# Second attention's causal masks in 32-row pieces on TensorE instead of whole 128-row products

## What is computed

```python
def _L1_attn_ref(x, w_qkv, w_proj):          # x: (16, 256, 128), H = 16, D = 8
    qkv = x @ w_qkv
    q, k, v = jnp.split(qkv, 3, axis=-1)     # then (B, H, T, D)
    att = jnp.einsum('bhqd,bhkd->bhqk', q, k) / sqrt(D)
    causal = jnp.tril(jnp.ones((T, T), dtype=bool))
    att = jnp.where(causal[None, None], att, jnp.finfo(att.dtype).min)
    att = jax.nn.softmax(att, axis=-1)
    y = jnp.einsum('bhqk,bhkd->bhqd', att, v)
    return y.transpose(0, 2, 1, 3).reshape(B, T, C) @ w_proj
```

## Time and profile before

| what | value |
|---|---|
| median of 3 runs | 992.38 us (991.43 to 995.08) |
| the profiled execution | 995.66 us, of which the span of instructions is 993.5 us |
| PE busy | 738.8 us (74%) |
| DVE, ACT, POOL busy | 646.1, 616.5, 457.2 us |
| mean granted TensorE clock | 0.861 of full speed |

### The profile page before, as it was taken

One profiled execution on the slowest core, in us unless ns is written; L12 is line 12 of the kernel. 1 busy time (PEld: TensorE's weight loads), 2 busy tenths in 40 slices (PEclk: granted clock), 3 DMA queues, 4 the chain that ended last, 5 costly groups with the idle time before them and its releaser, 6 DMA issues.

```text
span 993.5 us, 21325 instructions
## 1 busy us (share of the span) xinstructions
PE 738.8 (74%) x8182; PEld 570.7 (57%) x8182; DVE 646.1 (65%) x1190; ACT 616.5 (62%) x1139; POOL 457.2 (46%) x484
## 2 busy tenths in 40 slices
PE   6757777989888990577944777787888888888670
PEld 4445555878878880344632445555766766666540
DVE  5766655767667543777566555475777687688537
ACT  6653545766767462675632444575778878788765
POOL 5476653243443553110005665223566756666632
PEclk8769779999999996678875878698999999999965
DMA  9711112011111115200004222200111111111062
GB/s 312 303 45 54 62 54 60 20 53 31 47 46 39 50 44 149 66 1 2 1 1 156 89 83 69 75 12 23 33 39 38 44 34 39 39 34 31 19 186 85
DMA packets 62357, 63.81 MB, mean 64 GB/s; under 512 B 7378, under 2 KB 52322, under 8 KB 62132
## 3 DMA queue, kind: packets, MB, share of 16 engines
q1 hardware_dynamic: 53300, 44.02, 15.1%
q0 software_dynamic: 8960, 18.43, 5.7%
HBM read 31.88 MB, written 30.55 MB: 63 GB/s over the span
## 4 chain that ended last, share of the span: by engine, by line
PE 33%; ACT 19%; DVE 18%; issue 16%; POOL 8%; another core or an unknown queue 3%; DMA 2%; SPq 0%; ACTq 0%; POOLq 0%; DVEq 0%
POOL xs L1877 6%; PE bank L721 4%; ACT arena L1220 4%; ACT L881 3%; PE bank L786 3%; PE bank L798 3%; PE bank L675 3%; PE bank L528 2%; PE bank L691 2%; DVE arena L1737 2%; DVE arena L1644 2%; DVE arena L1624 2%; DVE arena L1642 1%; PE bank L800 1%
## 5 line engine op out<-in xcount | busy, mean ns | idle before, releaser
L1896 POOL DMA_INDIRECT ys<-arena x152 | 172.7, 1136 | 175.3 <-ACT arena L1149 56.1
L1877 POOL DMA_INDIRECT xs<-arena x128 | 134.0, 1047 | 74.3 <-issue 33.6
L1220 ACT ACTIVATE arena<-bank 128x512 f32<-128x512 f32 x192 | 98.9, 601 | 84.8 <-PE bank L786 59.0
L1737 DVE TENSOR_REDUCE arena<-bank 128x2 bf16<-128x512 f32 (+1 forms) x192 | 119.2, 683 | 41.7 <-PE bank L759 36.8
L661 PE MATMUL bank<-arena 128*128 128x128 bf16 x608 | 105.8, 220 | 6.4 <-DVE arena L1589 3.3
L662 PE MATMUL bank<-arena 128*128 128x128 bf16 x608 | 105.7, 220 | 0.0
L663 PE MATMUL bank<-arena 128*128 128x128 bf16 x608 | 105.7, 219 | 0.0
L881 ACT ACT_TABLE_LOAD x72 | 92.4, 1283 | 1.3
L1725 DVE SCALAR_TENSOR_TENSOR arena<-arena,bank 128x512 bf16<-128x512 bf16 x64 | 46.0, 745 | 72.1 <-ACT arena L1193 68.8
L721 PE MATMUL bank<-arena 128*128 128x256 f32 x256 | 68.5, 416 | 0.9 <-issue 0.9
L661 PEld LDWEIGHTS bank<-arena 128*128 x608 | 60.2, 99 | 9.4 <-issue 6.5
(11 more groups left out here) (236 smaller groups left out, 2051.5 us busy)
## 6 DMA issues: line engine op xcount, KB each, us to landing
xs<-arena SPq DMA_DIRECT2D x19, 516.0 KB, 11.1
arena<-xs SPq DMA_DIRECT2D x38, 258.0 KB
arena<-ys SPq DMA_DIRECT2D x32, 256.0 KB, 5.0
arena<-in_MF SPq DMA_DIRECT2D x8, 512.0 KB
ys<-arena POOLq DMA_INDIRECT x152
arena<-in_x SPq DMA_DIRECT2D x8, 256.0 KB, 5.2
arena<-in_W SPq DMA_DIRECT2D x8, 256.0 KB, 2.7
xs<-arena POOLq DMA_INDIRECT x128
```

Of the source, the lines that this page charges most:

```text
L1220: act(PT[kt_][:, i, gs[0]:gs[0] + len(gs), :], bank_of["s2", b, n, i][:, :].rearrange("p (g q) -> p g q", q=w), ACT.Exp, scale=8 ** -0.5). ...
L1737: red(negM[b % 2][:, u, 32 * i + gs[0]:32 * i + gs[0] + len(gs)], kv_, op=ALU.max, negate=True).then_inc(m_max.sem, 1)
L1877: eng.indirect_dma_start(xs[l][:, :], bass.IndirectOffsetOnAxis(ap=slot_i[l][:, m:m + 1], axis=0), xrow[:, t, :], None).then_inc(rows_move ...
L1896: eng.indirect_dma_start(ys[l][:, :], bass.IndirectOffsetOnAxis(ap=yid[g % 4][:, j:j + 1], axis=0), y[:, 128 * j:128 * j + 128], None).the ...
```

## The change

The mask of a bank is no longer one matmul with 128 rows and 128 columns of the array. It is added in pieces: 32 rows (those of head group i, so that the four banks use the four strips of rows) by 32 columns of the array (32 of the output's partitions), and only over the columns that have anything masked for these partitions. With the order of tokens above that makes five pieces in `s1_four` (widths 32, 64, 32, 64 and 128 in each block; the third and fourth are for the same 32 output partitions) and four in `s2_four` (32, 64, 96 and 128). The counting up of `m_s1` or `m_s2` hangs on the last piece of each bank. The two mask constants hold other patterns, side by side in `masks`, of the same size; they depend on the partition modulo 32 alone. All else is the same.

```diff
+S1_MASKS = ((96, 96, 192, 32), (64, 64, 192, 64), (0, 0, 96, 32), (0, 64, 128, 64), (32, 0, 64, 128))
+S2_MASKS = ((32, 32, 192, 32), (0, 0, 192, 64), (64, 0, 32, 96), (96, 0, 0, 128))
...
-        identb, trib, onesb, negb, negtb = (sb(128, BF16) for _ in range(5))
+        identb, trib, onesb = (sb(128, BF16) for _ in range(3))
+        masks = sb(256, BF16)
...
+            def masks_added(k, i, w, w0, parts):
+
+                r = slice(32 * i, 32 * i + 32)
+                kv_ = k[:, :].rearrange("p (n c) -> p n c", c=w)
+                for q, c, m, width in parts:
+                    j = mm(kv_[q:q + 32, :, w0 + c:w0 + c + width], identb[r, r], bc(masks[r, m:m + width], 1, [32, 512 // w, width]),
+                           start=False, stop=False)
+                return j
...
                 for i, k in four:
-                    kv_ = k[:, :].rearrange("p (n c) -> p n c", c=w)
-                    mm(kv_[:, :, w - 128:w], identb, bc(negb, 1, [128, len(gs), 128]), start=False).then_inc(m_s1.sem, 1)
+                    masks_added(k, i, w, w - 128, S1_MASKS).then_inc(m_s1.sem, 1)
...
                 for i, k in four:
-                    kv_ = k[:, :].rearrange("p (n c) -> p n c", c=w)
-                    mm(kv_[:, :, 0:128], identb, bc(negtb, 1, [128, len(gs), 128]), start=False).then_inc(m_s2.sem, 1)
+                    masks_added(k, i, w, 0, S2_MASKS).then_inc(m_s2.sem, 1)
...
-                for o, i in ((identb, ident), (negb, negm_c), (negtb, negm_r)):
+                for o, i in ((identb, ident), (masks[:, 0:128], negm_c), (masks[:, 128:256], negm_r)):
...
-           np.where(later, -1e30, 0.0), one * (8 - np.arange(8)), one * (16 - np.arange(16)),
-           one * (128 * np.arange(64)), one * np.arange(80), np.where(later.T, -1e30, 0.0), one * i[:, None],
+           np.where(one * (i < 96) + (i - 96 < i[:, None] % 32) > 0, -1e30, 0.0), one * (8 - np.arange(8)), one * (16 - np.arange(16)),
+           one * (128 * np.arange(64)), one * np.arange(80), np.where(one * ((i < 64) + (i >= 96)) + (i - 64 > i[:, None] % 32) > 0, -1e30, 0.0), one * i[:, None],
```

1 line of the change is left out of this document (removed).

## The result

The changed kernel takes 1024.17 us (1021.29 to 1024.9, 4 runs), the kernel before, beside it, 992.84 us (991.43 to 995.08, 4 runs): ratio 1.032, 95% interval 1.028 to 1.037. It is slower by 3%, where the prediction had it faster by 0.9% and a range up to 998.

What follows compares the result with a forecast made beforehand. No engine was full; TensorE was busy 74% of the span and had 33% of the chain. Gains of 9.9 and 2.1 us, 9 after deductions, took 995.66 to 986.7 us, and 3.3 us for the median gave 983.5; range 976 to 998.

Steps and rivals of the forecast that it cites:

- The cost of a round after: Mask rounds at 2.4 GHz, four blocks: `s2_four` 0.41 us for 0.87, `s1_four` 0.62 for 0.97; `s2_four` two blocks 0.30 for 0.44.
- the 0.1 us a round that I took for loads: `s1_four`: weight loads on a tile in use might add 0.2 us a round; half taken, 0.7 us off in all.
- Rivals 1 and 2: 1: a strip's column strips take turns, 1017 us, chance 0.06; 2: each piece costs its own issue, 1001 us, chance 0.07.
- The added 1344 matmuls and loads cost no issue time, by the 4 ns of the earlier trace: TensorE's mask rounds: the extra instructions were counted at nothing, since matmuls on different strips start 4 ns apart.
- rival 2: Each piece costs an issue of 0.055 us; two-block rounds lose from 16 ns steps, four-block from 38: 1001 us, chance 0.07.
- Handed on whole: Expert stage: the gain before 704.85 reaches DVE's copy at 713.00, idle 1.73 us for TensorE alone, without loss.
- The 12 us on the chain: Gain of mask rounds from which TensorE goes on in the chain of waits: 9.9 us in `s2_four`, 2.1 in `s1_four`.
- three rounds of the expert stage: DVE starts on the first mask only after the last, as something holds TensorE's signals; these rounds were counted at nothing.
- Rival 3: Gain not handed on: ACT and DVE as late in the expert stage, scatters set the stage before; 988 to 991 us, chance 0.22.
- rival 4: TensorE does less and waits more: stretches at 1.2 GHz or held signals eat the gain; 992 to 998 us, chance 0.11.
- What would show it: Signs in the changed trace: round times, start steps, turns still 12 us, PEclk below 0.77 and 0.98, or growing "remote" waits.
- The 0.16 for slower: Chance that the whole kernel measures slower by more than about 0.5%, 5 us.

Runs made afterwards that it cites:

- split_masks: Kernel before, each whole mask matmul cut along its columns into four slices (five in `s1_four`), same work and shape: 1016.77 us, ratio 1.019.
- split_again: Repeat of split_masks on one chip of the first sort, beside the changed kernel run again: 1017.78 us, ratio 1.023.
- half_masks: Kernel before, whole-array masks over only half of each bank's blocks, the other blocks unmasked: 1000.56 us, ratio 1.005.
- the quarter kernels: Kernel before, whole-array masks over a quarter of their columns, the rest unmasked; three runs: ratios 1.006, 1.008 and 1.007.
- quarter_third: Kernel before, whole-array masks over a quarter of their columns, the rest unmasked, on the second sort of chip: 954.22 us, ratio 1.007.
- pieces_scatter: Changed kernel's mask pieces for sequences 4 to 7 alone, whole masks elsewhere as in the kernel before, second sort of chip: 949.86 us, ratio 1.001.
- pieces_late: Changed kernel's mask pieces for sequences 8 to 15 alone, whole masks for 0 to 7, second sort of chip: 953.03 us, ratio 1.007.

## Why the prediction was wrong

- **The cost of a round after: right, and for most rounds too high.** 0.45 for my 0.41 with four blocks, 0.26 for 0.30 with two, 0.58 for 0.67 at 1.2 GHz; `s1_four` 0.38 for 0.62: of the two pieces on a shared tile the second does start 0.066 us after the first (427.857 and 427.923 us), but all four banks have that wait at the same time, where I had added it up bank by bank, and the 0.1 us a round that I took for loads isn't there. Rivals 1 and 2 are refuted wherever the instructions are there: rows and strips of columns start 3 to 4 ns apart alike. Here I had weighed the rule of the Trainium skill ("TensorE: Matmul & The Clock Gate", section on the mechanism of packing small matmuls) that a weight load overlaps only where the strip of rows differs; the thirteen starts in 50 ns, four on each of three strips of rows, disagree with it.
- **The step that failed first: "The added 1344 matmuls and loads cost no issue time, by the 4 ns of the earlier trace rows".** The 4 ns are the distance of instructions that TensorE already has. Whether it gets them is another question, and the row couldn't answer it. The trace of before had the answer in small: 3.2 us of waits for "issue" inside scores and maxima in the scatter stage, which no semaphore explains. The prediction doesn't mention them. The number of instructions costs 1.9 to 2.3% on the first sort of chip (split_masks, split_again). My point for rival 2, that steps of 16 ns eat the gain, was the right sort of worry with the wrong form: not each step is longer, but in nine rounds some are 0.7 to 1.15 us. In the expert stage no mask round of the changed kernel has a standstill; there the number costs split_masks 4.0 us by later signals, 2.08 us late for 1.29.
- **"Handed on whole": wrong.** The 12 us on the chain were counted in the trace of before, round by round. half_masks and the quarter kernels take up to three quarters of the columns away and win nothing, 252.7 to 253.4 us in the expert stage where the kernel before has 253.0. The chain passes through those rounds, but the signal of their masks comes when it comes, 9.31 and 9.37 us into the turn with masks that end 0.43 us apart. The prediction knew that something holds TensorE's signals back, and counted it for three rounds of the expert stage; 42 of the 168 mask signals there are late by more than 0.2 us. Rival 3 had the outcome right, with 0.22, but not the reason (ACT and DVE as late as TensorE); on the first sort of chip it is the time of before, not a gain of 4 us. On the second sort, without late signals, ten turns at 2.4 GHz take 138.7 us in quarter_third and 140.1 in pieces_scatter, so a little is handed on there.
- **The clock (rival 4): right mechanism, its size off by far, and its chance too low.** I gave it 992 to 998 us. By itself less work costs 0.5 to 0.8%, 998 to 1001 us, which is near. But I let it work on masks alone, 0.86 us a round. At 1.2 GHz everything on TensorE takes twice as long, above all the 96 up projections of a turn (608 of each of three lines in 19 turns) that the earlier trace rows show at 0.055 us, and these were beside the chain, not on it. The stage had 227.6 us of TensorE in 270, and that at 2.4 GHz; I should have seen that this leaves no room for the lower clock.
- **What would show it** did: PEclk below 0.77 and 0.98 in the stages was named as the sign of rival 4, and it is lower in all four stages. The held signals that rival 4 names beside the clock are there too, but no rival had the number of instructions as their cause.
- **Range and chances.** The range took every bound of the cost of a piece, and none for the supply of instructions, as no row priced it. The 0.16 for slower came from rivals 1, 2 and part of 4. A term for which the trace has no price and which the change makes 4.5 times as large (384 to 1728 instructions) should have had a case of its own.

What stays open: why TensorE's instructions stop. The standstills stand beside GpSimd's indirect transfers, in the profiles of the first sort and above all in those with more instructions, and are all but absent on the second, where the same transfers run. That the transfers cause them, or the late signals, wasn't tried apart. The whole program has 78 packets on its instruction queue for 68 before (1.28 MB for 1.11), which is ten more, so a standstill isn't one for each packet. Nor is it a packet under way: by the packets' times in the trace none moves on that queue from 501.4 to 543.0 us, with the standstill of 533.47 in between, and only one of the nine standstills has a packet beside it. The Trainium skill ("Runtime: NRT & Kernel Launch", section on the mechanics of instruction fetch) says that the sequencer fetches the next block of 256 instructions through a DMA queue of its own, and that this is mostly hidden; the packets agree with it (16 KB each, ten more for 2688 more matmuls and loads), and eight of nine standstills stand without a fetch to hide. Also open are what holds TensorE's signals, why more instructions make them later, and whether the 32x32 shape costs by itself.

## What to carry to other kernels

Splitting one matmul into small ones is paid in instructions, and that price isn't the distance of two starts: look for idle time that ends on "issue" inside unbroken groups of the kernel before, above all beside indirect transfers, and give it a case of its own. Before a gain on a producer is counted, look at how long after the producer's end its consumer starts: where that is 1.3 us and not 0.01, the gain has nowhere to go. Taking work from an engine that waits for others can slow its clock, and then the price is paid on everything else that this engine does in that stage; so first try what the removed work is worth by leaving it out (half_masks took one run to show that it was worth nothing). Compare on one chip, and on more than one, before a 1% difference is believed.

## What the runs showed of the hardware that I had not expected

- Matmuls of 32x32 on all sixteen tiles, each with its own weights, start 3 to 4 ns apart while they are supplied; thirteen within 50 ns.
- Standstills of 0.7 to 1.15 us between bunches of one to eight matmuls, 16.0 and 21.9 us in the first two attention stages of two profiles of the changed kernel on the first sort of chip, 1.6 us on the second.
- TensorE's semaphore signals come 0.014 us after a matmul's end on one sort of chip, and on the other often in a bunch: the first 1.29 us late in one turn of the kernel before, 2.08 with four times as many mask matmuls.
- The kernel before takes 996 to 1000 us on three chips and 947 us on two; the scatter stage makes up 18 us of it (119.4 us against 101.2 in pieces_late, whose masks are the old ones up to there).
- TensorE's clock, once down at 811.0 us, stayed at 1.2 GHz for 6.8 us though TensorE was busy for 6.64 of them; the kernel before, with the same idle stretches and longer masks, stayed at 2.4 GHz there, and from 693.6 to 935.9 us without a break.
